# TensorE makes the inflows of twelve states, two states at a time in 64x128 tiles, and dt is projected once with a ScalarE copy of its positive part, in a bidirectional state-space layer on one core

## The reference, cut to what matters

```python
dbc = u @ xproj_w.T
dt = jax.nn.softplus(dbc[..., :dt_rank] @ dt_w.T + dt_b)
Bm = dbc[..., dt_rank:dt_rank + d_state]
Cm = dbc[..., dt_rank + d_state:]
A = -jnp.exp(A_log)
dA = jnp.exp(dt[..., None] * A)
dBu = (dt * u)[..., None] * Bm[:, :, None, :]

def step(h, inp):
    dA_t, dBu_t, C_t = inp
    h = dA_t * h + dBu_t
    return (h, jnp.einsum('bdn,bn->bd', h, C_t))
```

## Time and profile before

| what | us |
|---|---|
| median of three executions | 1566.91 |
| lowest, highest | 1558.56, 1570.34 |
| the profiled execution | 1558.44 |
| its span from first to last instruction | 1556.6 |
| Mamba part in it (last out_project ends at about) | 972 |

### The profile page before, as it was taken

How to read it: one execution, slowest core, us unless ns; L and a number is a source line. 1 busy time by engine, 2 the same in 40 slices (tenths; PEclk the granted TensorE clock), 3 DMA queues, 4 the chain that set the end, 5 groups by cost and what they waited for, 6 DMA issues and landing times.

```text
span 1556.6 us, 43543 instructions
## 1 busy us (share of the span) xinstructions
PE 1347.9 (87%) x17914; PEld 1014.4 (65%) x17914; DVE 1161.2 (75%) x1926; ACT 958.4 (62%) x1750; POOL 1060.3 (68%) x684
## 2 busy tenths in 40 slices
PE   6798888889889989889889777898998999997595
PEld 3566766656756666666666666457997666666594
DVE  6788888888898887888888886523335888876376
ACT  6877777777766776876876765313555555542144
POOL 3798888888898888888888886340333466583552
PEclk9899999999999999999999989999999999999798
DMA  5122232232232222222222220531124200001223
GB/s 189 58 93 95 85 107 81 85 108 80 85 103 80 91 102 80 91 102 80 95 98 79 97 91 29 213 98 36 52 79 126 98 1 2 2 29 54 80 64 98
DMA packets 51604, 128.95 MB, mean 83 GB/s; under 512 B 8080, under 2 KB 33168, under 8 KB 41696
## 3 DMA queue, kind: packets, MB, share of 16 engines
q1 hardware_dynamic: 46640, 116.36, 21.8%
q0 software_dynamic: 4768, 9.81, 1.9%
HBM read 113.20 MB, written 18.56 MB: 85 GB/s over the span
## 4 chain that ended last, share of the span: by engine, by line
PE 52%; ACT 15%; DVE 15%; issue 8%; POOL 5%; another core or an unknown queue 2%; DMA 1%; SPq 1%; DVEq 0%; ACTq 0%; POOLq 0%
PE py L530 8%; PE pa L508 8%; DVE hh L925 5%; ACT da L723 4%; POOL hc L1077 3%; PE pr L1990 2%; PE bank L1536 2%; PE bank L1532 2%; PE bank L1546 2%; PE pq L413 2%; PE pq L385 2%; PE pr L2004 2%; ACT uz L625 2%; DVE hh L902 2%; PE pr L2193 2%
## 5 line engine op out<-in xcount | busy, mean ns | idle before, releaser
L1077 POOL TENSOR_TENSOR hc<-hh,cs 128x1024 f32<-128x1024 f32 x256 | 602.9, 2363 | 138.5 <-DVE hh L925 70.6
L925 DVE TENSOR_TENSOR_SCAN hh<-da,st,pa 128x512 f32<-128x512 f32 x240 | 293.6, 1266 | 65.5 <-PE pa L508 55.5
L508 PEld LDWEIGHTS pa<-dg,dtut 64*64 64x64 f32 x10240 | 180.8, 137 | 179.4 <-issue 175.6
L530 PE MATMUL py<-ident,hc 128*128 128x128 f32 x2048 | 277.1, 279 | 19.3 <-ACT yt L743 19.2
L508 PE MATMUL pa<-dg,dtut 64*64 64x64 f32 x10240 | 219.1, 226 | 80.9 <-DVE yz L934 38.5
L530 PEld LDWEIGHTS py<-ident,hc 128*128 128x128 f32 x2048 | 227.8, 142 | 44.7 <-ACT yt L743 21.2
L723 ACT ACTIVATE da<-dt,w 128x512 f32<-128x512 f32 x320 | 212.7, 711 | 11.3 <-DVE hh L925 10.4
L723 ACT ACTIVATE pa<-dt,w 128x512 f32<-128x512 f32 x192 | 127.7, 684 | 97.2 <-DVE hh L925 96.4
L925 DVE TENSOR_TENSOR_SCAN hh<-pa,st,hh 128x512 f32<-128x512 f32 x144 | 175.4, 1267 | 2.6 <-ACT pa L723 1.9
L385 PE MATMUL pq<-xn,w 128*128 128x512 f32 x248 | 121.0, 613 | 5.0 <-ACT xn L759 3.6
L925 DVE TENSOR_TENSOR_SCAN hh<-da,pa 128x512 f32<-128x512 f32 x80 | 93.2, 1207 | 29.4 <-PE pa L508 26.3
(11 more groups left out here) (349 smaller groups left out, 2807.8 us busy)
## 6 DMA issues: line engine op xcount, KB each, us to landing
cs<-bcrows SPq DMA_DIRECT2D x64, 1024.0 KB, 4.7
bs<-bcrows SPq DMA_DIRECT2D x32, 256.0 KB, 3.9
xsorted<-in_pads SPq DMA_DIRECT2D x13, 387.0 KB, 5.3
rot<-in_rot SPq DMA_DIRECT2D x4, 1024.0 KB, 5.0
wx<-in_l_w SPq DMA_DIRECT2D x4, 1024.0 KB, 10.3
ysort<-ytoken SPq DMA_DIRECT2D x14, 256.0 KB
wx<-in_l_w SPq DMA_DIRECT2D x1, 3072.0 KB, 12.3
wx<-in_l_w SPq DMA_DIRECT2D x1, 2304.0 KB, 16.7
```

Of the source, the lines that this page charges most:

```text
L508: i = pe.matmul(pa[turn["step", s, h] % SLOTS][c * HQ:(c + 1) * HQ, kt * P + r * HQ:kt * P + (r + 1) * HQ], dtut[rows, kt, h * P + c * HQ: ...
L530: i = pe.matmul(py[:, h * CH + kt * P:h * CH + (kt + 1) * P], hc[s % HCS][:, h, t], ident[:, :], is_transpose=True, start=n == 0 and kt == ...
L925: v.tensor_tensor_scan(hh[s % HHS][:, h, :], a, b, 0.0 if first else st[:, m % 2, n, h:h + 1], ALU.mult, ALU.add).then_inc(s_taken, 1)
L1077: g.tensor_tensor(hc[s % HCS][:, :, :], hh[s % HHS][:, :, :], cs[j % 2][:, s % CG, :].unsqueeze(1).broadcast_to([P, HF, CH]), ALU.mult).th ...
```

## The change

- `BY_G` is gone with its DMAs and buffer. `BY_V` becomes 6, 7, 12, 13, `BY_P` the other twelve, in the pairs (0,1), (2,3), (4,5), (8,9), (10,11), (14,15).
- For a pair, the step of its first state makes and scans half 0 of both states, the step of its second state half 1 of both (a "flow"). Eight matmuls of 64 rows x 128 columns, each with 2 x 64 moving columns, fill two neighbouring banks with the inflows of the two states, one column of the one beside one of the other; each scan reads every second column. A bank is free when both scans of its flow are done (`free`). There is one phase instead of two, and the adding-up stands behind it.
- So that a bank holds 256 consecutive tokens, `dtu` and B are turned with every fourth token together (`by_fours`).
- dt is projected once, over the 64 rows that hold its rank; the bias goes into ScalarE's instructions. ScalarE also keeps the positive part in `rx` (L649 becomes two instructions) and copies it into slots at step 11 (`relu_again`), in place of TensorE's `dt_again`. `finish` is a plain addition.
- `keep_state` comes two steps late instead of one. GpSimd makes six pairs of diagonals in a unit instead of five.

```diff
-BY_G = (0, 12)
-BY_V = (1, 6, 11, 13)
-BY_P = tuple(n for n in range(NS) if n not in BY_G + BY_V)
+BY_V = (6, 7, 12, 13)
+BY_P = tuple(n for n in range(NS) if n not in BY_V)
...
-                        order += [("step", s, h) for h in range(HF)]
+                        if n in BY_P:
+                            order += [("flow", pair_of(s), BY_P.index(n) % 2, j) for j in range(2)]
+                        else:
+                            order += [("step", s, h) for h in range(HF)]
...
+                def free(i):
+
+                    i -= SLOTS
+                    return i // 2 * 2 + 2 if handed_items[i][0] == "flow" else i + 1
...
+                def by_fours(t):
+
+                    return t.rearrange("p (j k) -> p k j", k=4)
...
-                            i = pe.transpose(pb[:, kt * P:(kt + 1) * P], dtu[m % 2][:, h, kt * P:(kt + 1) * P], ident[:, :])
+                            i = pe.transpose(pb[:, kt * P:(kt + 1) * P], by_fours(dtu[m % 2][:, h, :])[:, kt, :], ident[:, :])
...
+                        i = turn["flow", k, h, 0]
+                        pe.wait_ge(s_turnk, turned_count(m, 2))
+                        pe.wait_ge(s_dg, k + 1)
+                        if i >= SLOTS:
+                            pe.wait_ge(s_taken, free(i + 1))
                         for kt in range(4):
                             for r in range(2):
-                                h, rows = (r + phase) % 2, slice(r * HQ, (r + 1) * HQ)
-                                for c in range(2):
-                                    i = pe.matmul(pa[turn["step", s, h] % SLOTS][c * HQ:(c + 1) * HQ, kt * P + r * HQ:kt * P + (r + 1) * HQ],
-                                                  dtut[rows, kt, h * P + c * HQ:h * P + (c + 1) * HQ], dg[pair % DGS][rows, of, kt, :],
-                                                  start=True, stop=True)
-                        i.then_inc(s_pin, 1)
+                                rows = slice(r * HQ, (r + 1) * HQ)
+                                mm = pe.matmul(pa[i % SLOTS + r].rearrange("p (j k n) -> p k n j", n=2, k=4)[:, kt, :, :],
+                                               dtut[rows, kt, h * P:(h + 1) * P], dg[k % DGS][rows, :, kt, :], start=True, stop=True)
+                        mm.then_inc(s_pin, 1)
...
-                            if n == 12:
-                                dt_again(m)
...
+                        if s + 1 < STEPS and by_pe(s + 1) and n != 10:
+                            inflow(s + 1)
+                        if s + 2 < STEPS and by_vector(s + 2):
                             spread_b(s + 2)
...
                         prep(m + 1, n)
+                        if n == 10:
+                            inflow(s + 1)
...
-                        act.activation(ab[:, h, :], pq[:, :], ACT.Abs).then_inc(s_ra, 1)
+                        act.activation(rx[:, h, :], pq[:, :], ACT.Relu, bias=bias)
+                        act.activation(ab[:, h, :], pq[:, :], ACT.Abs, bias=bias).then_inc(s_ra, 1)
...
+                            v.wait_ge(s_pin, 2 * k + h + 1)
+                            for j, nj in enumerate(own):
+                                i, q = turn["flow", k, h, j], 4 * k + 2 * h + j
+                                v.wait_ge(s_slot, slot_count(i))
+                                inflows = pa2[i // 2 % (SLOTS // 2)][:, j::2]
+                                v.tensor_tensor_scan(hh[(NS * m + nj) % HHS][:, h, :], da[q % DAS][:, :], inflows,
+                                                     0.0 if first else st[:, m % 2, nj, h:h + 1], ALU.mult, ALU.add).then_inc(s_taken, 1)
```

More of the change, by code:

```diff
@@ L256, in layer0_mamba @@
                 pb = bank(k, "pb")
-                pa = [bank(k, f"pa{i}") for i in range(SLOTS)]
+                pa2 = [bank(k, f"pa{i}", 2) for i in range(SLOTS // 2)]
+                pa = [pa2[i // 2][:, i % 2 * CH:(i % 2 + 1) * CH] for i in range(SLOTS)]
                 pq = bank(k, "pq")
@@ L571, in mamba_tensor @@
                         turn_dtu(0, h)
[L572 removed]
+                    inflow(0)
                     for s in range(STEPS):
@@ L1086, in mamba_gpsimd @@
                     g.wait_ge(s_small, 96)
-                    inflow(0)
-                    b_diagonals(0)
+                    for k in range(2):
+                        b_diagonals(k)
                     for s in range(STEPS):
@@ L1092, in mamba_gpsimd @@
                             dt_times_u(m + 1)
-                        if s + 2 < STEPS and (s + 2) % NS in BY_G:
-                            inflow(s + 2)
-                        ahead = [k for k in range(1, UNITS * len(PAIRS)) if NS * (k // len(PAIRS)) + PAIRS[k % len(PAIRS)][0] == s + 4]
+                        ahead = [k for k in range(2, UNITS * len(PAIRS)) if NS * (k // len(PAIRS)) + PAIRS[k % len(PAIRS)][0] == s + 4]
                         for k in ahead:
```

204 lines of the change are left out of this document (83 added, 121 removed).

## The result

| | us |
|---|---|
| before, median of 4 (lowest to highest) | 1563.87 (1558.56 to 1570.34) |
| after, median of 4 (lowest to highest) | 1641.62 (1639.97 to 1647.84) |
| ratio, 95% interval | 1.0503 (1.0449 to 1.0556) |
| predicted | 1594 (1568 to 1650) |

What follows compares the result with a forecast made beforehand. No engine is full, so hand-overs bound it, chiefly VectorE waiting for TensorE's inflows. 0.6 + 0.6 + 1.14 = 2.3 us a unit, +32 over 14 units, +31 with start and end: 1589 or 1598, stated as 1594, range 1568 to 1650.

Steps and rivals of the forecast that it cites:

- One block of TensorE: TensorE's flow of eight matmuls: 1.07 us taken, bounds 0.94 and 1.9, against 1.24 for two old phases.
- The rival of slow writes: TensorE's flows writing every eighth float run at half speed, 1.9 us each, 8 us a unit: 1710 us; chance 12%.
- the fourth rival: VectorE's scans with a stride of two are slower: +50 to +200 us; chance 7%.
- The border: Between two units, scans wait for TensorE's inflows: scan 2 0.8 us late, scan 4 and step 5 0.6 late.
- Steps 5 and 6: `mid_part` and `low_part` come 0.6 us later, and VectorE's new inflow for state 7 puts 1.14 ahead of scan 6.
- Steps 7 to 10: TensorE, busy without a hole, brings the factor 0.7 to 0.8 us sooner; VectorE's inflow of 1.14 makes it 0.4 later net.
- Steps 12 and 13: Dropping `dt_again`, 1.8 us of TensorE, is worth nothing; ScalarE's copies are covered; GpSimd's change taken as 0.
- The relief of TensorE: Scan 1 starts right behind scan 0; a unit loses `dt_again`'s 1.8 us, 25 less: 1535 to 1540 us; chance 8%.

Runs made afterwards that it cites:

- the kernel with two fillers: The changed kernel plus sixteen useless TensorE transposes behind the prep of step 6 and sixteen behind that of step 12: 1570.49 us, ratio 1.0272.
- The fillers: Sixteen useless TensorE transposes added to the changed kernel behind the prep of step 6 (1621.82 us), then sixteen more behind that of step 12 (1570.49 us).
- the filler at step 12: Sixteen useless transposes behind the prep of step 12, added to the kernel before with dt projected only once: 1553.75 us, ratio 1.0163.
- the one at the gate: Sixteen useless transposes ahead of the flow of step 7, added to the kernel before with dt projected only once: 1537.39 us, ratio 1.0056.

## Why the prediction was right in direction and wrong in size

**One block of TensorE: right.** 1.09 us from a flow to its successor, 1.07 taken. The rival of slow writes falls: with every eighth float32 written a flow's row is 1.16, with the columns side by side 1.16. With it falls, for this kernel, the rule of the page Advanced Engine Details and Errata, section Memory Cachelines, of the Trainium skill, that any access to PSUM that isn't contiguous slows a matmul significantly. The scans at a stride of two take 1265 ns on average in after (the group above), those of before without a stride 1266: the fourth rival falls too.

**The border: nearly right.** The last copy of `dtut` to scan 3 was worked out as the place of the loss, with scans 0 to 2 in their places within half a microsecond. The silu's wait was missed: of the chain "keep, decays, table load, silu" I moved the z projection's end only, and not the adding-up of state 12, which the silu also needs. That is 1.15 us between scan 0 and scan 3 in the faster units. Scan 4, which was to wait for TensorE, follows scan 3 without a wait.

**Steps 5 and 6: VectorE right, TensorE left out.** In the faster unit at 416 us scan 0 to the end of scan 6 takes 26.4 us by the rows above (forecast 25.8). But the inflow for state 7 was priced as 1.14 us of VectorE alone. It also makes TensorE wait, for its bank and then for a slot behind four scans, and the step took every duration of TensorE from a profile at clock 0.99. This is the step that failed: the second inflow's price on TensorE's side, waits and half clock, was put at nothing. The place is the one that "Steps 7 to 10" of the prediction took as full: there the factor was to come 17.6 us behind the start of `low_part` (3.1 + 1.14 + 13.4), with no wait at scans 8 and 9. With the half clock it comes after 18.7 to 23.0 us, and scan 9 waits 1.45 us in the faster unit at 416 us and 3.60 in the slower one before it. Without it, in the kernel with two fillers, it comes after 17.3, and scan 9 waits 0.21. The fillers put a number on the whole: 63.5 to 61.5 to 60.5 us a unit. The clock is the 3 us a unit, some 42 us in 14 units, that were missing. That a unit with both fillers stands within 0.3 of the 60.2 worked out from the order is in part luck: the silu's wait was missed, and the factor comes 0.3 sooner than worked out.

**Steps 12 and 13: wrong.** "Worth nothing" for `dt_again`, and "it costs nothing" for ScalarE's passes in steps 7 and 8, were together 1.6% when that edit stands alone. 0.4 us a unit is there without any fall of the clock, and the rest comes by way of the clock: the idle piece at the gate then comes at moments at which it falls. How much of the 5% of the whole change is this edit's can't be told from that, since idle pieces and period are others there.

**The relief of TensorE** lost, as forecast: scan 1 does not stand directly behind scan 0. The experiments show what it needs: with VectorE's inflows at the border, where TensorE is late anyway, the same flows make the kernel 1.7% faster than before, with a filler 2.2%.

## What to carry to other kernels

Sum the idle pieces of TensorE beside the waits of the engine that sets the pace. A wait added to TensorE has a second price, the blocks behind it at half the clock, and this price can be as large as the wait (3.0 us behind one of 2.85 us, in the kernel that projects dt once and has its filler at step 12). Useless transposes in the gap are a test of it, and a cheap remedy if it is the right gap: the filler at step 12 of that kernel gave nothing, the one at the gate 1.0%. And ask of a kernel with an unusually even period what happens if it becomes half a microsecond longer: an edit that is "covered" may still cost 1.5%.

When work moves between engines, give the moved work to the place where the engine that lost it is late anyway.

## What the runs showed of the hardware that I had not expected

- TensorE's granted clock falls from 2.4 to 1.2 GHz behind idle pieces of 2 to 3 us within an otherwise full stretch, for about 3 to 10 us. A flow's row then reads 2.08 us and not 1.16, that of dt_project 2.07 and not 1.12.
- The same idle piece, with the same blocks around it, halves the clock in one unit and not in another. In the kernel before this hardly happened; 7.3 us of useless writes of VectorE brought it on and cost 23 us.
- A float32 write of every eighth element of a bank, and a scan that reads every second, cost nothing here: 1.16 us a flow's row either way, 1265 ns a scan and 1266 without the stride.
- 32 matmuls of 64x64 by 128 columns take no longer than 16 of 64x128: a row of 1.10 us against 1.16.
